# A decoder layer with routed experts on one core: leftover rows share three slots, and the orders of all engines are written anew

## The chip, the cores and the metric

The kernel runs on one core of one Trainium2 chip. The metric is device time in microseconds, the median of several runs; lower is better.

## The reference

The input x is 4 x 512 tokens of 512 channels. One layer computes three blocks, each followed by a layer norm over the channels.

```python
# block 1: a gated linear recurrence with quantised ("bitlinear") products
i = silu(bitlinear(x, Wi)) * (1 - f);  f = sigmoid(bitlinear(x, Wf))
h = scan over the tokens of a batch: h = f * h + i
o = rmsnorm(bitlinear(x, Wg)) * g_norm_weight * (h * sigmoid(h))
x = layernorm(x + bitlinear(o, Wo))
# block 2: each token goes to one of four experts, by its token id
e = min(token_id // 6250, 3)
x = layernorm(x + (silu(x @ ctx[e].T) * (x @ ctx[e].T)) @ ctx[e].T)
# block 3: eight square factors, which add up to one matrix
x = layernorm(x + (x @ sum_r factors[r]) / sqrt(8) + bias)
```

A bitlinear product rounds x per token to 8 bits and the weights to -1, 0 or 1. In block 2 the same matrix ctx[e] serves as gate, up and down weight.

## The kernel before

The 2048 tokens are 16 tiles of 128 rows, and 8 groups of two tiles. Block 1 runs group by group: `quantise_x`, `transpose_x`, three projections (`project_f`, `project_i`, `project_g`), the scans along the tokens on VectorE, `silu_h_by_token`, `output`, `quantise_o`, `transpose_o`, `project_back`, `residual_1`, `norm_1`. Then `scatter_rows` (GpSimd, an indirect DMA) writes each finished row with its token number to the DRAM array `sorted_rows`, at the row that `place` holds, so that the rows of one expert come to lie together.

Blocks 2 and 3 read `sorted_rows` slot by slot; a slot is 128 rows of one expert. As the four experts' row counts are no multiples of 128, the kernel has 19 slots (16 + 3). The first 13 (`SURE`) are always full. The last six may be part empty: they are first filled from `pad_row` by one large write, and rows that nothing was scattered to carry a token number out of bounds, so that `store` drops them. Which expert a slot has stands in `slot_off`, from which each expert product loads a register.

A slot n goes through: `load_rows` (SP queue; waits for the scatter of the groups that can reach it, the last group's for the last slots), `transpose_a` (PE), `high_a` and `low_a` (ACT and DVE split the transposed rows into a high and a low part), `up` (twelve matmuls 128x128 by 128x512: high by high, high by low, low by high), `silu_z` (ACT), `hidden` (DVE, silu(z) times z), `transpose_h`, `high_h`, `low_h`, `down` (twelve matmuls), `residual_2` (DVE), `square_2` (ACT), `power_2` (GpSimd), `norm_2` (ACT), `transpose_m`, `add_bias` (GpSimd), `high_m`, `low_m`, `mix` (twelve matmuls), `residual_3`, `square_3`, `power_3`, `norm_3`, and `store` (GpSimd, an indirect DMA to the output rows by token). The buffers for z, the hidden rows and the high and low parts exist once each; `rows` and `x2` are rings of four.

The routing is computed on the chip from the token ids at the start: counts per tile and expert by PE, running sums by DVE, and then `fill_events`, `number_slots`, `open_slots` and `places` as chains of small operations on GpSimd, each of which waits for the one before (`link`). `low_of_ctx` (DVE) and `high_of_ctx` (ACT) split the sixteen chunks of ctx; the first `up` waits for all sixteen.

The order of the work on each engine is written out by hand. The first groups are lists of calls. Three turns follow (groups 5 to 7 of block 1, with slots 3 to 8 beside them), then one turn with the last group's block-1 rest, and then the last stage, a loop over n from `TAIL` = 11 that issues up(n), transpose_a(n+1), transpose_m(n-2), down(n-1), transpose_h(n), mix(n-2). An engine works its list strictly in order, and semaphores hold it where an input isn't there or a buffer isn't free.

## Time and profile before

| what | value |
|---|---|
| median of 3 runs | 341.45 us (340.44 to 343.64) |
| profiled execution | 342.06 us |
| its span, first to last instruction | 340.3 us |
| PE busy | 278.1 us, 82% |
| DVE busy | 226.3 us, 66% |
| ACT busy | 229.6 us, 67% |
| POOL (GpSimd) busy | 190.8 us, 56% |
| mean granted clock of PE | 0.963 |

PE is the matmul engine (TensorE), PEld its weight load, which runs beside it. DVE is VectorE, ACT ScalarE, SP the engine that issues most DMAs. The span is a little shorter than the device time. A share of the whole span is an average over stages: which engine sets the pace has to be read stage by stage. In a timeline, the bracket behind an instruction tells how long its engine sat idle before it, and what ended that.

### The profile page before, as it was taken

Reading aid. Unit: us, or ns where it says so; the run is one execution under the profiler, and the core shown is the slowest. Engines: PE = TensorE matmul, PEld = TensorE weight load, DVE = VectorE, ACT = ScalarE, POOL = GpSimd, SP = SyncE. Lnnn points to the kernel's source line nnn. Section 1 sums busy time; section 2 is a strip of 40 time slices with the busy share of each in tenths; the row PEclk is TensorE's granted clock in tenths of the full one; section 3 lists DMA queues with packets and bytes.
Section 4 is the critical chain, followed back from the end, with each engine's and each line's share of the span. In section 5 each row is a group of like instructions: output and inputs, shape, how many; then the busy total and the mean of one; then the engine's idle time right before and its main releaser. Section 6 shows DMA issues by size and latency. Waiting matters only on the chain.

```text
span 340.3 us, 5734 instructions
## 1 busy us (share of the span) xinstructions
PE 278.1 (82%) x1505; PEld 211.9 (62%) x1518; DVE 226.3 (66%) x488; ACT 229.6 (67%) x456; POOL 190.8 (56%) x381
## 2 busy tenths in 40 slices
PE   1376646484879899999999998998999999999760
PEld 1253414252557678787778876676888888887540
DVE  2789999999987879968677696454543434543310
ACT  4687789889678769986887686476555644554530
...
DMA packets 17406, 37.02 MB, mean 109 GB/s; under 512 B 1503, under 2 KB 1631, under 8 KB 17376
## 3 DMA queue, kind: packets, MB, share of 16 engines
...
## 4 chain that ended last, share of the span: by engine, by line
PE 62%; ACT 9%; issue 5%; DVE 5%; DMA 2%; POOL 2%; ACTq 0%; POOLq 0%; DVEq 0%; SPq 0%
PE bank_y L1455 5%; PE bank_z L1455 5%; PE bank_y L1456 5%; PE bank_z L1456 5%; PE bank_z L1459 5%; PE bank_y L1459 5%; PE bank_m L1455 4%; PE bank_m L1456 4%; PE bank_m L1459 4%; PE bank_tr L1424 3%; PE bank_c L1357 2%; PE bank_q L1424 2%; PE bank_a L1357 1%; PE bank_b L1357 1%; DMA sorted_rows<-r,place 1%
## 5 line engine op out<-in xcount | busy, mean ns | idle before, releaser
L312 POOL TENSOR_SCALAR n_v<-n_dev 128x1 f32<-128x1 f32 (+1 forms) x46 | 8.8, 192 | 52.2 <-ACT x L644 26.7
L1455 PE MATMUL bank_y<-c_hi,h_hi 128*128 x76 | 31.8, 418 | 1.8 <-ACT h_hi L612 1.4
L996 DVE TENSOR_TENSOR act_z<-bank_z,act_z 128x512 f32<-128x512 f32 x19 | 13.1, 689 | 30.1 <-ACT act_z L626 30.1
L1455 PE MATMUL bank_m<-f_hi,m_hi 128*128 128x512 f32 x76 | 32.1, 423 | 0.8 <-ACT m_hi L612 0.8
L353 POOL TENSOR_TENSOR x<-x,bias_b 128x512 f32<-128x512 f32 x19 | 24.6, 1293 | 14.5 <-PE bank_q L1424 14.5
L1455 PE MATMUL bank_z<-c_hi,a_hi 128*128 x76 | 30.4, 400 | 2.8 <-ACT a_hi L612 1.5
L1456 PE MATMUL bank_m<-f_lo,m_hi 128*128 128x512 f32 x76 | 30.8, 405 | 0.0
L1456 PE MATMUL bank_y<-c_lo,h_hi 128*128 x76 | 30.1, 396 | 0.0
L1456 PE MATMUL bank_z<-c_lo,a_hi 128*128 x76 | 30.1, 395 | 0.0
L612 ACT ACTIVATE h_hi<-bank_tr 128x512 fp32r<-128x512 f32 x19 | 11.3, 596 | 26.7 <-PE bank_tr L1424 26.7
L313 POOL TENSOR_TENSOR n_d<-n_v,minus_half 128x1 f32<-128x1 f32 (+1 forms) x46 | 27.1, 588 | 3.8
L358 POOL DMA_INDIRECT out<-r,token_of x19 | 20.3, 1067 | 12.3 <-ACT r L651 7.6
L1013 DVE SCALAR_TENSOR_TENSOR r<-bank_m,x 128x512 f32<-128x512 f32 x19 | 13.1, 691 | 21.0 <-PE bank_m L1459 20.0
L1002 DVE SCALAR_TENSOR_TENSOR x<-bank_y,rows 128x512 f32<-128x512 f32 x19 | 13.1, 691 | 19.1 <-PE bank_y L1459 19.1
L638 ACT ACTIVATE x<-x,n_b,n_d 128x512 f32<-128x512 f32 x19 | 15.4, 810 | 12.2 <-POOL n_b L314 12.2
L1357 PE MATMUL bank_c<-xq_t,w_q 128*128 128x256 bf16 x128 | 18.3, 291 | 5.2 <-ACT mc_row L540 2.7
L343 POOL DMA_INDIRECT sorted_rows<-r,place x16 | 17.8, 1113 | 8.3 <-ACT r L594 5.7
L1459 PE MATMUL bank_m<-f_hi,m_lo 128*128 128x512 f32 x76 | 21.3, 403 | 0.0
L1459 PE MATMUL bank_y<-c_hi,h_lo 128*128 x76 | 20.6, 393 | 0.0
L1459 PE MATMUL bank_z<-c_hi,a_lo 128*128 x76 | 20.6, 393 | 0.0
L644 ACT ACTIVATE x<-r,n_mean 128x512 f32<-128x512 f32 x19 | 13.7, 720 | 9.6 <-DVE n_mean L1017 9.6
L626 ACT ACTIVATE act_z<-bank_z 128x512 f32<-128x512 f32 x19 | 11.2, 592 | 12.1 <-PE bank_z L1459 12.1
...
## 6 DMA issues: line engine op xcount, KB each, us to landing
...
```

The costliest lines, as they stand in the source:

```text
L313: link(pool.tensor_tensor(d, v, minus_half[:, 0:v.shape[1]], ALU.pow), chain)
L343: pool.indirect_dma_start(sorted_rows, bass.IndirectOffsetOnAxis(place[:, u:u + 1], 0), r1[:, j, :], None).then_inc(s_scat[j], 16)
L353: pool.tensor_tensor(tile, tile, bias_b[:], ALU.add).then_inc(s.x2b, 1)
L358: pool.indirect_dma_start(out_rows, bass.IndirectOffsetOnAxis(token_of[:, n:n + 1], 0), r3[:, n % 2, :], None, bounds_check=B * S - 1, oob ...
L638: a.activation(r, r, ACT.Identity, bias=n2_b[:, n % 2:n % 2 + 1], scale=n2_d[:, n % 2:n % 2 + 1]).then_inc(s.x2, 1)
L644: a.activation(x2[:, n % RING, :], r3[:, n % 2, :], ACT.Square, bias=n3_mean[:, n % 2:n % 2 + 1], accum_out=n3_dev[:, n % 2:n % 2 + 1]).th ...
L996: v.tensor_tensor(act_z[:], bank_z[:], act_z[:], ALU.mult).then_inc(s.hid, 1)
L1357: last = t.matmul(bank[:, i * GW:(i + 1) * GW], w_q[:, m, d, ch:ch + P], xq_t[:, :, d, :], start=(d == 0), stop=(d == KC - 1))
L1424: last = t.transpose(bank[:, c * P:(c + 1) * P], src[:, c * P:(c + 1) * P], ident[:])
L1455: t.matmul(bank[:], hi[:, c, :], w_hi(c), start=(c == 0), stop=False)
L1456: t.matmul(bank[:], hi[:, c, :], w_lo(c), start=False, stop=False)
L1459: last = t.matmul(bank[:], lo[:, c, :], w_hi(c), start=False, stop=(c == KC - 1))
```

## The change

The last six slots are replaced by three. Each of the three holds rows of two experts: GpSimd sorts the four leftover counts (`sort_left`), computes where each expert's leftover rows start and where they jump (`share_slots`), and which expert and which mask each of the six "units" has (`share_units`). There are then 16 slots and 19 units. A shared slot has one transpose_a, two ups, two hiddens with a mask per row, two transposes of h and two downs that add into one bank, and one residual_2, transpose_m and mix. The padding and its write are gone. Ahead of and behind that, the order of the calls is changed on all five engines, in the first groups and in the turns; the last stage is written out call by call. `sort_left` has 14 linked operations, `share_slots` 12, `share_units` 10, `places` 25 in place of 14. The diff follows, cut, in the order constants, SP, GpSimd, ACT, DVE, PE; of the orders of the first groups only stretches are shown.

```diff
-N_SLOTS = N_TILES + N_EXPERTS - 1
 SURE = N_TILES - N_EXPERTS + 1
+SHARED = N_TILES - SURE
+N_UNITS = SURE + 2 * SHARED
...
+def units_to(n):
+    return n + 1 if n < SURE else SURE + 2 * (n - SURE + 1)
+def slot_of(unit):
+    return unit if unit < SURE else SURE + (unit - SURE) // 2
+def is_last(unit):
+    return 0 <= unit < N_UNITS and units_to(slot_of(unit)) == unit + 1
...
-                sp.wait_ge(s.pad, 2)
-                sp.dma_start(sorted_rows[SURE * P:, :].rearrange("(k p) c -> p k c", p=P),
-                             pad_row[:, None, :].to_broadcast([P, N_SLOTS - SURE, ROW])).then_inc(s.padded, 16)
...
+                def sum_of_four(out, a, scratch):
+                    link(pool.tensor_tensor(scratch, a(slice(0, 2)), a(slice(2, 4)), ALU.add), s.route)
+                    link(pool.tensor_tensor(out, a(slice(0, 1)), a(slice(1, 2)), ALU.add), s.route)
+                def sort_left():
+                    expert = consts[:, 0:N_EXPERTS]
+                    square = [P, N_EXPERTS, N_EXPERTS]
+                    left = unsorted[:, 0, :]
+                    link(pool.tensor_scalar(unsorted[:, 1, :], expert, float(KC), None, ALU.mult), s.route)
+                    pool.wait_ge(s.left, 2)
+                    link(pool.tensor_scalar(sure_rows[:], sure_rows[:], float(P), None, ALU.mult), s.route)
+                    link(pool.tensor_tensor(left, through[:, :, N_TILES], sure_rows[:], ALU.subtract), s.route)
+                    link(pool.tensor_scalar(size_key[:], left, float(N_EXPERTS), None, ALU.mult), s.route)
+                    link(pool.tensor_tensor(size_key[:], size_key[:], expert, ALU.add), s.route)
+                    link(pool.tensor_tensor(pairs[:], size_key[:, :, None].to_broadcast(square),
+                                            size_key[:, None, :].to_broadcast(square), ALU.subtract), s.route)
+                    link(pool.tensor_scalar(pairs[:], pairs[:], 1.0, None, ALU.is_ge), s.route)
+                    sum_of_four(size_rank[:, :, None], lambda c: pairs[:, :, c], pairs[:, :, 0:2])
+                    link(pool.tensor_tensor(at_rank[:], size_rank[:, None, :].to_broadcast(square),
+                                            expert[:, :, None].to_broadcast(square), ALU.subtract), s.route)
+                    link(pool.tensor_scalar(at_rank[:], at_rank[:], 0.0, None, ALU.is_equal), s.route)
...
+                    sum_of_four(by_size[:, :, :, None], lambda c: sorted_pairs[:, :, :, c], sorted_pairs[:, :, :, 0:2])
+                def share_slots():
+                    square = [P, N_EXPERTS, N_EXPERTS]
+                    first, second, third = (by_size[:, k, 0:1] for k in range(3))
+                    link(pool.tensor_scalar(third_cut[:], second, -float(P), None, ALU.add), s.route)
+                    link(pool.tensor_scalar(third_over[:], third, P + 1.0, third, ALU.is_ge, ALU.mult), s.route)
+                    link(pool.tensor_scalar(jump[:], third, P + 1.0, third_cut[:], ALU.is_ge, ALU.mult), s.route)
+                    link(pool.tensor_scalar(base[:, 2:3], jump[:], SURE * P + 2.0 * P, None, ALU.add), s.route)
...
+                    sum_of_four(base_of[:, :, None], lambda c: pairs[:, :, c], pairs[:, :, 0:2])
+                def share_units():
+                    third, at = by_size[:, 2, 0:1], by_size[:, :, 1]
+                    link(pool.tensor_scalar(sizes[:, 0:2], by_size[:, 0:2, 0], 1.0, None, ALU.mult), s.route)
+                    link(pool.tensor_tensor(sizes[:, 2:3], third, jump[:], ALU.add), s.route)
+                    link(pool.tensor_scalar(shared_mask[:, 0:2 * SHARED:2], sizes[:], row_no, 1.0, ALU.subtract, ALU.is_ge),
+                         s.route)
...
+                    pool.tensor_scalar(shared_off[:], off_f[:], 1.0, None, ALU.mult).then_inc(s.shared, 1)
+                    pool.tensor_scalar(shared_mask[:, 1:2 * SHARED:2], shared_mask[:, 0:2 * SHARED:2], -1.0, 1.0, ALU.mult,
+                                       ALU.add).then_inc(s.shared, 1)
...
                     pool.wait_ge(s.next_fill, 6)
+                    link(pool.tensor_tensor(spare[:], through[:, :, 0:N_TILES], in_tile[:, 0, :, :], ALU.add), s.route)
                     link(pool.tensor_scalar(pos[:], filled[:, :, 0:N_TILES], -float(P), None, ALU.mult), s.route)
-                    link(pool.tensor_tensor(pos[:], pos[:], through[:, :, 0:N_TILES], ALU.add), s.route)
-                    link(pool.tensor_tensor(pos[:], pos[:], in_tile[:, 0, :, :], ALU.add), s.route)
+                    link(pool.tensor_tensor(pos[:], pos[:], spare[:], ALU.add), s.route)
                     link(pool.tensor_scalar(over[:], pos[:], float(P), None, ALU.is_ge), s.route)
                     link(pool.tensor_tensor(shift[:], later, now, ALU.subtract), s.route)
                     link(pool.tensor_scalar(shift[:], shift[:], float(P), -float(P), ALU.mult, ALU.add), s.route)
@@ -399,6 +477,20 @@
                     link(pool.tensor_scalar(placed[:], now, float(P), None, ALU.mult), s.route)
                     link(pool.tensor_tensor(placed[:], placed[:], pos[:], ALU.add), s.route)
                     link(pool.tensor_tensor(placed[:], placed[:], shift[:], ALU.add), s.route)
+                    wide = [P, N_EXPERTS, N_TILES]
+                    link(pool.tensor_tensor(spare[:], spare[:], sure_rows[:, :, None].to_broadcast(wide), ALU.subtract),
+                         s.route)
+                    link(pool.tensor_scalar(step[:], spare[:], jumps[:, 0:1], jumps[:, 1:2], ALU.is_ge, ALU.mult), s.route)
+                    link(pool.tensor_scalar(shared_at[:], spare[:], jumps[:, 2:3], jumps[:, 3:4], ALU.is_ge, ALU.mult), s.route)
+                    link(pool.tensor_tensor(step[:], step[:], shared_at[:], ALU.add), s.route)
+                    link(pool.tensor_tensor(step[:], step[:], at_rank[:, N_EXPERTS - 1, :, None].to_broadcast(wide), ALU.mult),
+                         s.route)
+                    link(pool.tensor_tensor(shared_at[:], spare[:], base_of[:, :, None].to_broadcast(wide), ALU.add), s.route)
+                    link(pool.tensor_tensor(shared_at[:], shared_at[:], step[:], ALU.add), s.route)
+                    link(pool.tensor_tensor(shared_at[:], shared_at[:], placed[:], ALU.subtract), s.route)
+                    link(pool.tensor_scalar(spare[:], spare[:], 0.0, None, ALU.is_ge), s.route)
+                    link(pool.tensor_tensor(shared_at[:], shared_at[:], spare[:], ALU.mult), s.route)
+                    link(pool.tensor_tensor(placed[:], placed[:], shared_at[:], ALU.add), s.route)
                     link(pool.tensor_tensor(placed[:], placed[:], chosen[:], ALU.mult), s.route)
...
                 number_slots()
+                open_slots()
                 weight_ready(W_F)
                 weight_ready(W_I)
-                open_slots()
+                sort_left()
                 weight_ready(W_G)
-                places()
-                add_factor(1)
+                share_slots()
                 scale_g(0)
                 power_x(2)
+                places()
                 scale_o(0)
+                add_factor(1)
                 weight_ready(W_O)
-                scale_g(1)
                 power_x(3)
                 number_rows(0)
...
-                scale_g(2)
+                share_units()
                 power_x(4)
...
                 square_x(1, 1)
                 weight_sum(W_F)
                 weight_sum(W_I)
+                max_row(0)
+                weight_sum(W_G)
+                weight_ready(W_F)
                 x_by_channel(0)
-                max_row(0)
-                weight_ready(W_F)
-                weight_sum(W_G)
                 weight_sum(W_O)
                 weight_ready(W_I)
                 tanh_f(0, 0)
-                forget(0, 0)
+                square_x(2, 0)
+                square_x(2, 1)
                 weight_ready(W_G)
                 silu_i(0, 0)
-                square_x(2, 0)
+                forget(0, 0)
+                high_of_ctx(0, range(0, 1))
+                tanh_f(0, 1)
                 square_g(0, 0)
+                silu_i(0, 1)
+                forget(0, 1)
+                max_row(1)
+                high_of_ctx(0, range(1, 2))
+                square_g(0, 1)
                 x_by_channel(1)
...
+                high_m(14)
+                square_3(13)
+                square_2(15)
+                norm_3(13)
+                square_3(14)
+                norm_2(15)
+                high_m(15)
+                norm_3(14)
+                square_3(15)
+                norm_3(15)
...
                     dve.wait_ge(s.sz, n + 1)
-                    v.tensor_tensor(act_z[:], bank_z[:], act_z[:], ALU.mult).then_inc(s.hid, 1)
+                    if n < SURE:
+                        v.tensor_tensor(act_z[:], bank_z[:], act_z[:], ALU.mult).then_inc(s.hid, 1)
+                    else:
+                        dve.wait_ge(s.shared, 2)
+                        v.scalar_tensor_tensor(act_z[:], bank_z[:], shared_mask[:, n - SURE:n - SURE + 1], act_z[:], ALU.mult,
+                                               ALU.mult).then_inc(s.hid, 1)
                 def residual_2(n):
                     i = slice(n % 2, n % 2 + 1)
-                    dve.wait_ge(s.y, n + 1)
+                    dve.wait_ge(s.y, units_to(n))
...
+                def sure_fills():
+                    dve.wait_ge(s.numbers, 1)
+                    v.scalar_tensor_tensor(sure_fill[:], number[:], float(SURE), gain[:], ALU.is_lt, ALU.mult
+                                           ).then_inc(s.left, 1)
+                    dve.wait_ge(s.left, 1)
+                    v.tensor_reduce(sure_rows[:], sure_fill[:].rearrange("p t e -> p e t"), AX, ALU.add).then_inc(s.left, 1)
...
+                quantise_x(2)
                 max_x(3, 0)
-                output(0, 0)
-                rescale_f(1, 0)
-                output(0, 1)
-                max_o(0, 0)
-                rescale_i(1, 0)
-                rescale_i(1, 1)
-                rescale_f(1, 1)
-                max_o(0, 1)
-                scale_x(2)
-                quantise_x(2)
-                round_weights(W_O)
+                weigh_g(1, 0)
+                scans(1, 0)
                 quantise_o(0)
-                gate_i(1, 0)
-                weigh_g(1, 0)
                 max_x(3, 1)
-                slot_offsets()
-                low_of_ctx([0])
-                scans(1, 0)
+                weigh_g(1, 1)
                 gate_i(1, 1)
-                low_of_ctx([1])
-                weigh_g(1, 1)
+                low_of_ctx([2])
+                scans(1, 1)
                 residual_1(0)
-                scans(1, 1)
+                low_of_ctx(range(3, 5))
                 rescale_f(2, 0)
...
+                residual_1(1)
+                output(2, 0)
+                rescale_f(3, 0)
+                rescale_f(3, 1)
+                output(2, 1)
...
                 residual_1(2)
+                low_of_ctx([13])
                 output(3, 0)
-                low_of_ctx(range(13, 15))
+                low_of_ctx([14])
+                max_x(5, 1)
+                low_of_ctx([15])
                 output(3, 1)
+                low_a(0)
                 rescale_f(4, 0)
-                max_x(5, 0)
-                low_of_ctx([15])
+                scale_x(5)
+                max_o(3, 0)
+                max_o(3, 1)
+                hidden(0)
...
+                def expert_product(unit, n, bank, hi, lo, s_hi, s_lo, s_done, first=True, last=True):
+                    if unit < SURE:
+                        off = slot_off[0:1, unit:unit + 1]
+                    else:
+                        pe.wait_ge(s.shared, 2)
+                        off = shared_off[0:1, unit - SURE:unit - SURE + 1]
+                    at = pe.value_load(off, min_val=0, max_val=(N_EXPERTS - 1) * KC)
                     product(n, bank, hi, lo, lambda c: flat(c_hi[:, bass.ds(at + c, 1), :]),
-                            lambda c: flat(c_lo[:, bass.ds(at + c, 1), :]), s_hi, s_lo, s_done)
+                            lambda c: flat(c_lo[:, bass.ds(at + c, 1), :]), s_hi, s_lo, s_done, first, last)
                 def up(n):
                     after(pe, s.hid, n)
@@ -1470,35 +1670,37 @@
                         pe.wait_ge(s.split_dve, N_EXPERTS * KC)
                         pe.wait_ge(s.slot_off, 1)
                         pe.wait_ge(s.o, GT * (MERGE - 1) + 1)
-                    expert_product(n, bank_z, a_hi, a_lo, s.tah, s.tal, s.z)
+                    expert_product(n, slot_of(n), bank_z, a_hi, a_lo, s.tah, s.tal, s.z)
                 def down(n):
-                    after(pe, s.r2, n)
-                    expert_product(n, bank_y, h_hi, h_lo, s.thh, s.thl, s.y)
+                    first = n < SURE or not is_last(n)
+                    if first:
+                        after(pe, s.r2, slot_of(n))
+                    expert_product(n, n, bank_y, h_hi, h_lo, s.thh, s.thl, s.y, first, is_last(n))
...
                 silu_h_by_token(3)
+                transpose_a(0)
                 project_f(4)
-                transpose_a(0)
+                up(0)
                 project_i(4)
-                up(0)
+                transpose_h(0)
                 project_g(4)
-                transpose_h(0)
                 pe.wait_ge(s.oqt, 3)
                 transpose_x(5)
-                spread_max(5)
                 pe.wait_ge(s.o, GT * MERGE)
                 down(0)
                 transpose_a(1)
+                spread_max(5)
                 pe.wait_ge(s.xqt, 6)
                 transpose_o(3)
                 up(1)
...
-                mix(TAIL - 3)
-                transpose_h(TAIL - 1)
-                transpose_a(TAIL)
-                for n in range(TAIL, N_SLOTS + 2):
...
+                mix(8)
+                transpose_a(11)
+                transpose_m(9)
+                transpose_h(10)
+                up(11)
+                transpose_a(12)
+                down(10)
+                transpose_h(11)
+                mix(9)
+                up(12)
+                transpose_a(13)
+                transpose_m(10)
+                down(11)
+                mix(10)
+                transpose_a(14)
+                transpose_h(12)
+                up(13)
+                transpose_m(11)
+                down(12)
+                transpose_h(13)
+                up(14)
+                mix(11)
+                down(13)
+                transpose_h(14)
+                transpose_m(12)
+                transpose_a(15)
+                up(15)
+                mix(12)
+                transpose_h(15)
+                down(14)
+                up(16)
+                down(15)
+                transpose_m(13)
+                up(17)
+                transpose_h(16)
+                mix(13)
+                down(16)
+                transpose_h(17)
+                up(18)
+                down(17)
+                transpose_h(18)
+                transpose_m(14)
+                down(18)
+                mix(14)
+                transpose_m(15)
+                mix(15)
```

## Rows read from the trace of the kernel before

**Rows 1.** Busy time by stage: length, busy PE, PEld, DVE, ACT, POOL; clock, DMA share, GB/s.
```profile
27.00:97.20 70.20, 43.16 (x281) 26.79 (x283) 68.86 (x140) 59.78 (x128) 47.66 (x82) 0.90 0.80 182
97.20:237.60 140.40, 134.68 (x746) 104.39 (x755) 100.60 (x212) 104.19 (x212) 88.63 (x183) 1.00 0.28 79
237.60:308.50 70.90, 70.90 (x350) 58.39 (x351) 31.43 (x74) 37.23 (x72) 32.05 (x65) 1.00 0.15 51
308.50:340.30 31.80, 18.22 (x76) 13.59 (x74) 7.63 (x20) 11.38 (x21) 12.99 (x23) 0.82 0.03 10
```

**Rows 2.** The same view for one slot of the last stage.
```profile
249.40:259.08 9.68, 9.68 (x50) 7.99 (x49) 4.29 (x10) 5.22 (x10) 4.48 (x9) 1.00 0.18 57
```

**Rows 3.** The chain that ended last (start, us, what), steady last stage.
```profile
246.61 0.94 PE bank_m L1459 x4
249.40 0.93 PE bank_z L1459 x4
```

**Rows 4.** The same chain, where the last group's rows come back from memory.
```profile
229.30 3.94 DMA sorted_rows<-r,place
233.32 2.62 DMA rows<-sorted_rows
236.16 0.67 PE bank_a L1424 x4
```

**Rows 5.** The chain again, in the drain behind the last up product.
```profile
307.57 0.93 PE bank_z L1459 x4
...
324.86 0.47 PE bank_m L1455
328.08 1.38 PE bank_m L1459 x4
```

**Rows 6.** Timeline of PE at up(11) (start, us, engine, line, operation; idle before it).
```profile
237.60 0.49 PE L1455 MATMUL bank_z<-c_hi,a_hi 128*128 x1 [0.78 <-ACT a_hi L612]
```

**Rows 7.** The chain at unit 1: silu, then hidden.
```profile
110.78 0.61 ACT act_z L626
111.41 0.70 DVE act_z L996
```

**Rows 8.** Timeline of PE in the first 120 us.
```profile
49.39 1.89 PE L1419 MATMUL bank_m<-w_q,oq_t 128*128 128x512 bf16 x4 [1.48 <-DVE slot_off L1085]
...
97.19 0.49 PE L1455 MATMUL bank_z<-c_hi,a_hi 128*128 x1 [1.33 <-issue]
...
107.70 0.49 PE L1455 MATMUL bank_z<-c_hi,a_hi 128*128 x1 [0.36 <-ACT a_hi L612]
...
112.16 0.66 PE L1424 MATMUL bank_tr<-small,act_z 128*128 128x128 f32 x4 [0.98 <-DVE act_z L996]
```

**Rows 9.** Timeline of ACT: the second square of g in group 0.
```profile
34.81 0.59 ACT L561 ACTIVATE squares<-bank_b 128x512 bf16<-128x512 f32 x1
```

**Rows 10.** Timeline of POOL in the first 70 us.
```profile
28.84 0.38 POOL L392 TENSOR_SCALAR pos<-filled 128x64 f32<-128x64 f32 x1 [1.25 <-DVE slot_at L1080]
29.30 0.31 POOL L393 TENSOR_TENSOR pos<-pos,through 128x64 f32<-128x64 f32 x1
...
30.10 0.81 POOL L395 TENSOR_SCALAR over<-pos 128x64 f32<-128x64 f32 x1
...
35.98 0.20 POOL L405 CAST place<-place_f 128x16 int32<-128x16 f32 x1
...
42.51 1.93 POOL L282 TENSOR_TENSOR o_rc<-o_mc,minus_one 128x2 f32<-128x2 f32 x1
...
62.89 0.21 POOL L277 TENSOR_TENSOR o_v<-o_ms,g_u 128x2 f32<-128x2 f32 x1
...
64.75 0.72 POOL L282 TENSOR_TENSOR o_rc<-o_mc,minus_one 128x2 f32<-128x2 f32 x1
```

**Rows 11.** Timeline of DVE: quantising o of group 0, the last low part.
```profile
45.76 1.70 DVE L902 TENSOR_SCALAR o_tok<-o_tok,o_q 128x512 f32<-128x512 f32 x2
...
94.97 0.68 DVE L1022 TENSOR_TENSOR c_lo<-c_stage,c_hi 128x512 fp32r<-128x512 f32 x1
```

681 lines of the change are left out of this document (383 added, 298 removed).

## The prediction

> **What bounds the kernel now.** I read the busy time by stage first [rows 1]. The reader is to see four regimes. From 27 to 97 us VectorE (DVE) is busy 68.86 of 70.20 us and TensorE (PE) only 43.16: DVE sets the pace. From 97.2 to 237.6 us PE is busy 134.68 of 140.40, and from 237.6 to 308.5 us it never stops (70.90 of 70.90, granted clock 1.00). In the last 31.80 us PE works 18.22: one slot's chain of dependences is left over. So PE work saved behind 97 us shortens the kernel one for one, and each microsecond DVE loses ahead of 97 us delays everything behind it.
>
> In the steady last stage a slot takes 9.68 us, all PE [rows 2]. One product of twelve matmuls takes 249.40 - 246.61 = 2.79 us [rows 3]. Three products are 8.37, so the three groups of four transposes take 9.68 - 8.37 = 1.31, or 0.44 each.
>
> **Part 1, three mixes fewer.** Up and down products stay 19 each (13 sure slots, and two experts in each of three shared ones). Three times a transpose of a, a transpose of m and a mix go: 3 x (2.79 + 2 x 0.44) = 11.0 us of PE. It comes out in two places.
> - From the first read of slot 11 (236.16 [rows 4]) to the end of the last up (307.57 + 0.93 = 308.5 [rows 5]) there are 22 products and 22 groups of transposes before, 20 and 18 after: -(2 x 2.79 + 4 x 0.44) = -7.3. The new order puts the transposes of m(9) and h(10) between transpose a(11) and up(11), which fills the 0.78 us of [rows 6]: together -8.1.
> - From 308.5 to the end at 340.3 one product and one group of transposes go: -3.2. Against it, norm_2(15) is now issued behind square_3(14), which waits for mix(14), although its own inputs come earlier: I add 0.3. The last mix runs from 324.86 to 328.08 + 1.38 = 329.46, 4.60 us where others take 2.79, after a wait [rows 5]; the granted clock of the stage is 0.82 [rows 1]. The new one stands behind a similar wait, and I keep 4.60. Together -2.9.
>
> The tail gives -11.0. Does its new order stall? One unit needs, between its up and its down, silu and hidden (0.61 + 0.70 and their waits, about 1.4 [rows 7]), a transpose, and the two splits of the same shape (about 1.3). The order has a product of 2.79 us over each: down(n-1) or a mix over silu and hidden, the next up over the splits. I walked units 11 to 18 with these durations and found one wait of 0.2 us. ACT and DVE have room (5.22 and 4.29 of 9.68 [rows 2]). The masked multiply in hidden has the shape of the plain one, and costs the same. SP must load slot 15 after token_of_row(11), which POOL now does behind power_2(12): the load lands about 2 us before its transpose. The register load ahead of each product is covered by four queued transposes; without that cover it costs up to the 1.33 us of [rows 8].
>
> **Part 2, the routing on POOL.** sort_left is 14 small operations, share_slots 12, share_units 10, and places grows from 14 to 25: 47 more, each waited for. sort_left stands in the gap ahead of weight_ready(W_G), where DVE is rounding that weight: nothing. share_slots stands before scale_g(0), which must wait for the second square of g anyway (34.81 [rows 9]): nothing. share_units comes near 70 us, where POOL waits for residual 1: nothing. Without that cover these three cost 36 x 0.39 (the shortest row and its gap) = 14 us on POOL.
>
> places is the exposed one: it now stands between power_x(2) and scale_o(0), where it was ahead of both. Its 14 operations took 35.98 + 0.20 - 28.84 = 7.3 us, 0.52 each; a 128x64 operation takes between 0.31 and 0.81 [rows 10]. Bounds for eleven more: 11 x 0.39 = 4.3 and 11 x 0.90 = 9.9; I take 0.52, the mean of their own neighbours, 5.8. So places takes 13.1, and 1.7 more as DVE rounds W_O meanwhile: in that stretch before, o_rc took 1.93 instead of 0.72 [rows 10]. It starts near 35.1 (the squares of g, then power_x(2)) and ends at 49.9; scale_o(0) needs 64.75 + 1.0 - 62.89 = 2.9, so o's scale is there at 52.8.
>
> The Trainium skill (SBUF — State Buffer, "SBUF: two separate sides") says that VectorE and GpSimd share one port pair under an exclusive lock, the loser being blocked for the whole operation. The trace agrees for o_rc (1.93 against 0.72). Taken for every operation of places, the rule gives about 350; with the neighbours' mean, the sum below.
>
> **Part 3, the front's new order.** quantise_o(0) began on DVE at 45.76 [rows 11]. The new order puts 4.2 us more in front of it (gate 0.6, two scans 1.3, a weighing 0.6, two low parts 1.2, slot offsets 0.1, sure_fills 0.4), so DVE arrives at 50.1 and waits for 52.8: +2.7 (bounds 0 and 7). Behind it: project_back(0) needs POOL's half of W_O, which now follows scale_o(0) and add_factor(1), hence starts near 55.5, and its two halves take 1.9 and 1.5 [rows 8]: DVE waits 1.0 in residual_1(0). output(2,0) now follows residual_1(1) directly, where a rescale stood between, and waits for PE's transposes: 0.8. Up to the last low part of ctx, which ended at 95.65 [rows 11] and releases up(0), the DVE work is 0.2 shorter (one more max_x and sure_fills; one output and one rescale fewer). DVE lag: 2.7 + 1.0 + 0.8 - 0.2 = 4.3.
>
> PE: up(0) moves ahead of project_i(4), 8 + 8 matmuls of 0.87 us a half, which used to run while PE waited for that low part: +1.75 of work behind the gate. In return it and the new order fill waits of 0.36 and 0.98 [rows 8]: -1.3. The front costs 4.3 + 1.75 - 1.3 = +4.75. In 97 to 237 us I change nothing: the same work, PE idle 5.7 in all; the gate by the last group's rows (3.94 + 2.62 us of DMA [rows 4]) moves along.
>
> The 1.5 MB of padding written at the start go, and with them a wait of scatter_rows(0) that was long over: 0, for nothing in the PE or DVE waits names that transfer.
>
> **Sum.** Span 340.3 - 11.0 + 4.75 = 334.05. The profiled execution took 342.06, 1.76 outside its span: 335.8. The median shown (341.45) is 0.6 below it: 335.2.
>
> **Rivals.** A measurement of this kernel can tell about 1% from no change.
> - A, the front absorbs the routing. places runs at its lower bound and nothing collides (POOL 4 us earlier, oq_s before DVE arrives), and the two later waits vanish with it. Then the front costs about 0.3, and the span is 340.3 - 11.0 + 0.3 = 329.6: 330.8. If the last mix also keeps the full clock, 329. For it: DVE has no other wait in [rows 1]'s second stage. Against: W_O behind add_factor is in the order.
> - B, the shared stage stalls. Units of one slot share act_z, bank_z, bank_tr and h, each single; if the register load shows at half of the 12 products of the shared units (6 x 1.33 = 8.0 less the 2 of lag it could absorb), the time is about 341. For it: 1.33 us stood bare before up(0) [rows 8]. Against: no gap at all in 22 products of the last stage [rows 1].
> - C, slower. The lock: every operation of places, and share_slots ahead of it, takes 0.92 with its gap (0.81 and up was seen [rows 10]). places then takes 23.0 instead of 13.1 and share_slots pushes its start by 12 x 0.53 less 1.5 of slack, 4.9: DVE waits 14.8 longer, and the time is 350. It decides from 6 us over my value, where the gain is used up.
> - That the saved work isn't on the path: excluded by 70.90 of 70.90 [rows 1].
>
> **How the numbers follow.** The forecast as told (331.8 to 338) 0.52, A 0.25, cases between it and no change (B, or half of C) 0.15, C or B in full, beyond 1% slower, 0.08. So faster 0.78, same 0.14, slower 0.08. The range takes in A with the full clock and B: 328.5 to 341.
>
> **What would show it.** Right: 16 mixes and 38 expert products; up(0) near 101 to 102 instead of 97.2; a DVE wait for POOL's o_q of 2 to 3 us before quantise_o(0); PE without gap from the first read of slot 11 to the last up, in about 64 us instead of 72.3; about 29 us from there to the end. Wrong in the front: up(0) at 98 or before. Wrong in the tail: PE gaps before bank_z or bank_y in the last 50 us, released by h_hi, act_z or nothing visible. The forecast falls if the middle stage loses more than it did before, for which I have no row.

## The result, and the profile after

The changed kernel takes 343.33 us (median of 20 runs, 340.92 to 346.41), the kernel before 341.51 us beside it (20 runs): a ratio of 1.0052, 95% interval 1.0032 to 1.0072. The forecast was 335.2 us in a range of 328.5 to 341, faster with a chance of 0.78. It was wrong: the change gains nothing and loses about 1.8 us. The times are medians of all executions; the ratios and their 95% intervals leave out executions that took over 1.5% longer than a kernel's fastest.

One thing has to be known before the trace is read. The profiled execution of the changed kernel took 341.05 us (span 339.2), 2.3 us under its own median, and the profiled one of before 342.06, 0.6 over its own. By the two traces the changed kernel is 1.1 us shorter, by the medians 1.8 us longer. So the trace shows where the forecast failed, but some 3 us of the loss at the median lie outside what it can show. The record has one thing on them. The mean granted clock of PE over an execution goes with the time: the six longest executions of the changed kernel (344.8 to 346.4 us) have 0.914 to 0.920, the six shortest (340.9 to 342.2) 0.923 to 0.946, and before has 0.963 in its profiled execution and 0.95 at the median of its later ones. Where in the kernel the clock differs, and whether it makes the time or follows it, no run shows.

The busy time by stage of the changed kernel (length, busy PE, PEld, DVE, ACT, POOL, clock, DMA share, GB/s); the cuts are up(0), transpose a(11) and about the last down product. The first stage answers to the first one of [rows 1]; the second ends at transpose a(11), where the one in [rows 1] goes on to up(11), so the stretch to hold beside it is 236.16 - 97.19 = 138.97:

```profile
27.00:103.77 76.77, 43.82 (x271) 27.25 (x269) 70.18 (x140) 59.05 (x123) 59.13 (x116) 0.82 0.57 137
103.77:245.33 141.56, 135.11 (x763) 104.76 (x763) 100.12 (x211) 104.80 (x212) 89.00 (x180) 1.00 0.29 78
245.33:316.80 71.47, 70.91 (x345) 58.08 (x346) 27.78 (x61) 30.83 (x60) 25.70 (x51) 1.00 0.11 38
316.80:339.20 22.40, 7.88 (x28) 5.55 (x27) 3.25 (x10) 6.08 (x11) 8.03 (x15) 0.72 0.09 35
```

The reader is to see that up(0) comes at 103.77 instead of 97.19 [rows 8], that DVE, which had 1.3 us idle in the front's stage [rows 1], has 6.6 now, and that PE still never stops for long in the 71 us from transpose a(11) on.

The chain that ended last, at the last group's rows and in the drain (start, us, what; it answers to [rows 4, 5]):

```profile
238.76 3.65 DMA sorted_rows<-r,place
242.49 2.79 DMA rows<-sorted_rows
245.33 0.66 PE bank_a L1619 x4
...
308.85 0.93 PE bank_z L1654 x4
...
323.54 0.76 PE bank_m L1650
327.06 0.95 PE bank_m L1654 x4
```

From transpose a(11) to the end of the last up product it is 309.78 - 245.33 = 64.45 us, where it was 308.5 - 236.16 = 72.34 [rows 4, 5]: -7.9. From there to the end it is 29.4 us for 31.8: -2.4. The saving is all there. Transpose a(11) itself comes at 245.33 instead of 236.16, 9.2 us later: 6.6 of it up to up(0), 2.6 in the stage between.

The same chain between the front and up(1) shows a path that before's chain doesn't take:

```profile
105.55 6.39 DMA sorted_rows<-r,place
112.00 2.67 DMA rows<-sorted_rows
...
116.65 0.49 PE bank_z L1650
```

The scatter of group 2 takes 6.39 us where the last group's took 3.65; an accumulate of the factors was issued at 98.49, 7 us ahead of it. PE had other work meanwhile and stood 0.70 us for these rows and 0.61 before up(1), so in this trace the path costs PE at most 1.3 us.

DVE's timeline in the front (start, us, engine, line, operation, and in brackets the idle time before it and what ended it), the answer to [rows 11]:

```profile
22.97 0.69 DVE L1069 TENSOR_TENSOR t_ch<-bank_c,mc_row 128x512 f32<-128x512 f32 x1 [1.46 <-PE bank_c L1552]
24.67 0.69 DVE L1069 TENSOR_TENSOR t_ch<-bank_a,mc_row 128x512 f32<-128x512 f32 x1 [1.02 <-PE bank_a L1552]
...
54.32 0.91 DVE L1057 TENSOR_SCALAR o_tok<-o_tok,o_q 128x512 f32<-128x512 f32 x2 [2.97 <-POOL o_q L304]
...
60.82 0.75 DVE L1123 SCALAR_TENSOR_TENSOR r<-bank_tr,o_a,xs 128x512 f32<-128x512 f32 x1 [0.55 <-PE bank_tr L1614]
...
79.91 0.69 DVE L1107 TENSOR_TENSOR o_tok<-o_tok,bank_z 128x512 f32<-128x512 f32 x1 [0.86 <-PE bank_z L1598]
...
91.95 0.97 DVE L1057 TENSOR_SCALAR o_tok<-o_tok,o_q 128x512 f32<-128x512 f32 x2 [1.49 <-POOL o_q L304]
...
101.75 0.68 DVE L1182 TENSOR_TENSOR c_lo<-c_stage,c_hi 128x512 fp32r<-128x512 f32 x1
```

The three waits that were forecast are there, nearly to size (2.97, 0.55 and 0.86 for 2.7, 1.0 and 0.8). Three that were not are there too: 1.46 and 1.02 at the first rescales, 1.49 at quantise_o(2). POOL's timeline shows the stretch of places, and what stood before quantise_o(2) (it answers to [rows 10]):

```profile
37.62 0.31 POOL L470 TENSOR_TENSOR spare<-through,in_tile 128x64 f32<-128x64 f32 x1
...
42.92 3.04 POOL L484 TENSOR_SCALAR shared_at<-spare,jumps 128x64 f32<-128x64 f32 x1
...
51.43 0.20 POOL L497 CAST place<-place_f 128x16 int32<-128x16 f32 x1
...
85.61 1.40 POOL L327 DMA_DIRECT2D f_sum<-in_factors  x1 [1.50 <-DMA f_sum<-in_factors]
...
88.11 2.41 POOL L300 TENSOR_TENSOR o_mf<-o_max,o_r 128x2 f32<-128x2 f32 x1
```

places took 51.63 - 37.62 = 14.0 us where 14.8 were forecast, though it began 2.5 us later. Two steps of 0.2 and 0.6 us stretch to 2.4 and 3.0 where DVE issues several operations back to back.

### The profile page after: what moved, and what is told of

The parts are those of the page before. It is cut to its first block, busy times and chain, and to the rows that moved or that the text cites. A ratio compares the mean times of both kernels' runs of the same rounds, so it can differ in the third digit from the quotient of the medians.

```text
span 339.2 us, 5554 instructions
## 1 busy us (share of the span) xinstructions
PE 267.8 (79%) x1458; PEld 203.7 (60%) x1458; DVE 218.4 (64%) x466; ACT 217.8 (64%) x432; POOL 198.6 (59%) x401
## 4 chain that ended last, share of the span: by engine, by line
PE 56%; POOL 17%; DMA 9%; issue 7%; ACT 5%; DVE 4%; SPq 0%; POOLq 0%; DVEq 0%; ACTq 0%
PE bank_z L1650 5%; PE bank_y L1650 5%; PE bank_z L1654 5%; PE bank_y L1654 5%; PE bank_z L1651 5%; PE bank_y L1651 5%; PE bank_m L1650 4%; PE bank_m L1651 4%; PE bank_m L1654 4%; PE bank_tr L1619 4%; DMA sorted_rows<-r,place 3%; DMA f_sum<-in_factors 3%; DMA xs<-in_x 2%; DMA rows<-sorted_rows 2%; PE bank_c L1552 2%
## 5 line engine op out<-in xcount | busy, mean ns | idle before, releaser
L373 POOL TENSOR_TENSOR x<-x,bias_b 128x512 f32<-128x512 f32 x16 | 20.6, 1286 | 14.1 <-PE bank_q L1619 14.1
L1650 PE MATMUL bank_m<-f_hi,m_hi 128*128 128x512 f32 x64 | 27.1, 424 | 0.8 <-ACT m_hi L728 0.8
L333 POOL TENSOR_TENSOR n_d<-n_v,minus_half 128x1 f32<-128x1 f32 (+1 forms) x40 | 23.9, 598 | 3.4
L1651 PE MATMUL bank_m<-f_lo,m_hi 128*128 128x512 f32 x64 | 25.9, 404 | 0.0
L378 POOL DMA_INDIRECT out<-r,token_of x16 | 17.3, 1081 | 12.8 <-ACT r L767 7.2
L1162 DVE SCALAR_TENSOR_TENSOR x<-bank_y,rows 128x512 f32<-128x512 f32 x16 | 11.0, 689 | 20.0 <-PE bank_y L1654 20.0
L1138 DVE TENSOR_TENSOR m_lo<-bank_q,m_hi 128x512 fp32r<-128x512 f32 x16 | 11.0, 689 | 16.4 <-ACT m_hi L728 16.4
L1650 PEld LDWEIGHTS bank_z<-c_hi,a_hi 128*128 128x128 f32 x76 | 14.3, 188 | 7.4 <-issue 4.6
L1138 DVE TENSOR_TENSOR h_lo<-bank_tr,h_hi 128x512 fp32r<-128x512 f32 x19 | 13.0, 686 | 8.2 <-ACT h_hi L728 8.2
L1650 PEld LDWEIGHTS bank_y<-c_hi,h_hi 128*128 128x128 f32 x76 | 14.3, 188 | 6.5 <-issue 3.5
```

The source lines that it names most:

```text
L333: link(pool.tensor_tensor(d, v, minus_half[:, 0:v.shape[1]], ALU.pow), chain)
L373: pool.tensor_tensor(tile, tile, bias_b[:], ALU.add).then_inc(s.x2b, 1)
L378: pool.indirect_dma_start(out_rows, bass.IndirectOffsetOnAxis(token_of[:, n:n + 1], 0), r3[:, n % 2, :], None, bounds_check=B * S - 1, oob ...
L1138: v.tensor_tensor(flat(lo[:]), bank[:], flat(hi[:]).bitcast(F32), ALU.subtract).then_inc(s_done, 1)
L1650: t.matmul(bank[:], hi[:, c, :], w_hi(c), start=(first and c == 0), stop=False)
L1651: t.matmul(bank[:], hi[:, c, :], w_lo(c), start=False, stop=False)
```

## The experiments

Two explanations are held against each other. **Theory 1**: GpSimd's added steps and the accumulates of the factors that they push back cost the front what it lost. **The order**: the new lists that came with the change cost by themselves (in the expectations of old_front_new_pool, no_share and no_share_old this is the other case, or the rival). Theories 2 and 3 in two expectations are smaller ones, on the accumulates and on one wait, and are told with their runs. Each kernel is timed against the kernel before on its own chip. In the tables "up(0)" and "a(11)" are the starts of the first up product and of transpose a(11) in the profiled execution; before has 97.2 and 236.2, the changed kernel 103.8 and 245.3. From a(11) to the end of the span all kernels with the new end took 93.9 to 95.5 us, so the two columns hold most of what the traces differ by; the medians can differ by more.

### Moving single things within the changed kernel

**places_split**: the last 15 steps of places behind scale_g(1).

```diff
                 power_x(3)
                 number_rows(0)
                 scale_g(1)
+                places_b()
```

> The changed kernel with one thing moved: the last fifteen operations of places run behind scale_g(1), not ahead of scale_o(0). Theory 1: the DVE wait of 2.97 us before quantise_o(0) goes (o's scale is there near 50 at the latest), and later waits decide: 1.5 us for o's scale in group 2 stays. up(0) near 101 to 102 instead of 103.8, ratio to before about 0.995. If the places chain doesn't matter because other waits are behind it, ratio as the changed kernel, 1.005.

Measured: 343.63 us, ratio 1.0041 (1.001 to 1.0072); up(0) 104.2, a(11) 246.5. The wait at quantise_o(0) went, as theory 1 has it, but quantise_o(1) now waited 2.4 us, the wait at quantise_o(2) rose to 2.3, and residual 1 waited 1.1 us for the scatter. Nothing was won: what leaves one wait arrives at the next.

**factor_later**: one accumulate of the factors (1 MB) behind scale_o(2), right ahead of scatter_rows(1).

```diff
-                add_factor(4)
                 scale_o(2)
+                add_factor(4)
                 scatter_rows(1)
```

> The changed kernel with add_factor(4) behind scale_o(2). In the changed kernel GpSimd stood 1.5 us at add_factor(4), for the DMA of the factor before, and then 2.4 us in one operation of scale_o(2) under a run of DVE operations with two SBUF inputs; DVE waited 1.5 us for the result. Theory 1: with scale_o(2) issued first its operation lies ahead of that run, the DVE wait goes, up(0) 1.5 to 2.5 us earlier, ratio to before about 0.999 to 1.000. Rival: another wait stands right behind (rows of slot 0 or PE), and less than 0.5 us is won.

Measured: 352.29 us, ratio 1.0309 (1.0255 to 1.0364); up(0) 114.4. The chain shows it:

```profile
91.44 1.49 POOL f_sum L327
93.23 1.12 POOL sorted_rows L363
94.66 8.24 DMA sorted_rows<-r,place
102.99 7.19 DMA rows<-sorted_rows
110.22 1.12 PE bank_tr L1619 x4
```

Scatter and load of the rows take 15.4 us where the last group's took 3.94 + 2.62 [rows 4]. DVE stood 5.8 us for that scatter at the next residual 1. An accumulate issued right ahead of them costs some 9 us over the changed kernel: one line in the list is worth as much as the whole change.

**factors_early**: every accumulate one place earlier, none ahead of scale_o(2).

```diff
+                add_factor(1)
                 scale_g(0)
                 power_x(2)
                 places()
                 scale_o(0)
-                add_factor(1)
+                add_factor(2)
...
-                add_factor(4)
                 scale_o(2)
```

> The changed kernel with the accumulates of the factors each one place earlier on GpSimd's queue: the first leaves ahead of places at 35 us in place of 54.5, the second at 54, the third at 65, the fourth at 75, and none ahead of the second group's output scale at 85.6, where GpSimd waited 1.50 us, or beside the scatter of group 1. Theory 2 (the late chain of 1 MB accumulates is what delays the start of the expert stage): up(0) 2 to 3 us earlier, 338 to 341 us. Rival (the accumulates are only passengers, the cost is GpSimd's and VectorE's own work): 342.5 to 344 us, up(0) at 103 to 104 us.

Measured: 343.0 us, ratio 1.0029 (0.9995 to 1.0063); up(0) 104.6, a(11) 245.5. The wait at quantise_o(2) is gone and the one at quantise_o(0) is 4.1 us for 2.97. The rival's time was right, and the accumulate ahead of scale_o(2) was a passenger. The run doesn't clear the one ahead of scatter_rows(2): it still leaves at 99.18, and the scatter behind it still takes 6.30 us.

**low_apart**: three low parts behind quantise_o(2).

```diff
-                low_of_ctx(range(8, 11))
                 quantise_o(2)
+                low_of_ctx(range(8, 11))
```

> The changed kernel with the three low parts of the context that stand ahead of quantise_o(2) set behind it. Theory 3 (three low parts back to back with the gate hold GpSimd's o_mf for 2.4 us, which is the 1.49 us wait of quantise_o(2)): quantise_o(2) starts 1 to 2 us earlier and group 1 and 2 with it, 341.5 to 342.5 us. Rival (the last low parts are what up(0) waits for, and their sum stays): 343 to 344 us.

Measured: 342.36 us, ratio 0.9999 (0.9964 to 1.0034); up(0) 104.8, a(11) 244.8. The mechanism of theory 3 held:

```profile
88.60 0.25 POOL L300 TENSOR_TENSOR o_mf<-o_max,o_r 128x2 f32<-128x2 f32 x1
90.29 0.97 DVE L1057 TENSOR_SCALAR o_tok<-o_tok,o_q 128x512 f32<-128x512 f32 x2 [1.49 <-POOL o_q L304]
```

o_mf takes 0.25 us where it took 2.41, and quantise_o(2) starts at 90.29 instead of 91.95. DVE's wait there is 1.49 as before, since DVE, without the low parts, arrives earlier too; and up(0) is no earlier, as the rival has it: the low parts still have to be done. The plain medians, 342.36 against 341.13, give a ratio of 1.0036. The interval reaches into that of the changed kernel, and it isn't a shown gain.

### The added steps under the order of before

**old_front_new_pool**: the lists of before for ACT, DVE and PE in the front, and for all engines in the turns; POOL's front as changed.

```diff
 ACT, DVE, PE: lists of before, sure_fills behind weight_scale(W_I)
 POOL: list of the changed kernel; turns of before
```

> As the kernel before in the calls of ACT, DVE and PE up to slot 10, with the changed kernel's order on GpSimd in the first groups (places between power_x(2) and scale_o(0)), and the new last stage. If GpSimd's new order alone makes the front slow, the old order of the others, which wants o's scale at 45.8, waits longer than the new one did: DVE waits 6 to 8 us before quantise_o(0), up(0) at 104 to 106, ratio 1.00 to 1.02. If the new order of ACT, DVE and PE makes it slow, up(0) is at 99 to 101 and the ratio 0.98 to 0.99.

Measured: 351.04 us, ratio 1.0251 (1.0201 to 1.03); up(0) 111.7, a(11) 255.5. The wait before quantise_o(0) is there with 5.8 us, a little under the forecast; up(0) is 6 us later than either case allowed, and DVE also waits 4.7 us for ACT's i_ch at 94.6 us.

**old_front2**: the lists of before on all engines, the added steps set into POOL's waits.

```diff
                 number_slots()
+                sort_left()            # nine of its steps
                 weight_ready(W_F)
+                sort_left_b()
+                open_slots()
                 weight_ready(W_I)
-                open_slots()
+                share_slots()
                 weight_ready(W_G)
                 places()               # its first ten steps
                 add_factor(1)
...
                 scale_g(1)
+                places_b()             # the other fifteen
```

> The order lists of the kernel before, front and turns, on all engines, with the changed kernel's end; the added scalar steps of GpSimd are set where it waited for the weights' rounding and behind group 1's gate, the last 15 steps of places behind scale_g(1), and the first accumulate of the factors leaves at 36 us as before. Theory 1 (GpSimd's added steps in front of group 0's output quantiser, with the accumulates of the factors pushed back behind them, cost the front): up(0) comes back to 97 to 99 us and the time to 331 to 334 us. Rival 1 (the added steps cost wherever they stand, since GpSimd is held by VectorE's port anyway): up(0) at 101 to 104 us, 337 to 343 us. Rival 2 (the changed order of ScalarE, VectorE and TensorE is itself needed by the shorter end): the middle stage stays at 141.5 us, the time at 336 to 340 us.

Measured: 343.59 us, ratio 1.0083 (1.0055 to 1.0111); up(0) 109.4, a(11) 247.7. Theory 1's forecast fails, and rival 1 fits better, though up(0) is later than it said too: with the lists of before the steps cost 12.2 us at up(0), though they were put into POOL's waits. DVE's timeline shows the first of it, in a gap that had looked free:

```profile
24.28 0.69 DVE L1076 TENSOR_TENSOR t_ch<-bank_c,mc_row 128x512 f32<-128x512 f32 x1 [3.87 <-PE bank_c L1560]
```

The largest others are 3.21 us for power_x(3), which stands behind places_b, and 1.27 and 2.99 for ACT's i_ch.

**before_plus11**: the kernel before with eleven more steps of 128x64 in places, and nothing else.

```diff
                 placed = placed + shift
+                extra[0] = placed * chosen
+                ten more of the same shape, each waited for
                 placed = placed * chosen
```

> The kernel before, with eleven more linked operations of 128x64 in places, whose result nobody reads: about 11 x 0.55 = 6 us more on GpSimd at 35 us, nothing else changed. If GpSimd's length there passes to the end one for one: 346 to 348 us, up(0) at 102 to 103 us. If only what is over the slack passes (1.9 us of wait at the first output scale and 5.6 us of idle time behind it): 342 to 345 us. If the slack takes it all: 341.5 us.

Measured: 344.92 us, ratio 1.0109 (1.007 to 1.0147); up(0) 101.7, a(11) 240.1. The 11 steps took 4.6 us of POOL (35.20 to 39.78) where 6 were expected, and they move up(0) by 4.5 and the time by 3.7 us: nearly one for one. Waits and idle time of POOL on both sides (over 7 us) took in little of it. The time lies in the range of the second case, but the slack is not what made it so.

**spread** and **spread2**: the same lists of before, with the steps spread from 22 to 67 us, and scatter_rows(0) behind scale_o(1). spread2 differs in the accumulates alone (and power_x(3) and power_1(0) moved up).

```diff
                 weight_ready(W_I)
                 open_slots()
+                sort_left()
                 weight_ready(W_G)
+                sort_left_b()
...
                 weight_ready(W_O)
+                share_slots()
...
+                places_b()
+                places_c()
                 scale_o(1)
+                add_factor(3)          # spread2; spread: behind power_x(4)
                 scatter_rows(0)
...
+                add_factor(4)          # spread2
                 scale_o(2)
                 scatter_rows(1)
-                add_factor(4)          # spread
```

> All the computation of the changed kernel, with the order of the kernel before on ScalarE, VectorE and TensorE (front and turns) and the changed kernel's end. The added steps stand where GpSimd has nothing due: the sort behind open_slots and behind W_G's half, share_slots and the last fifteen steps of places in the stretch from 47 to 64 us, scatter_rows(0) behind group 1's output scale, share_units behind the last scatter of the front; the accumulates leave at about 36, 51, 72, 86, 100, 108 and 117 us. If what the changed kernel lost is the changed order of the lists, and the added steps can be hidden: up(0) at 98 to 101 us, middle stage 138.5, 332 to 336 us, and it beats both kernels. If GpSimd's added steps cost wherever they stand (old_front2 had up(0) at 109.4): 339 to 344 us.

> As spread, with the accumulates of the factors kept away from the loads of the sorted rows (in spread two left at 90.2 and 105.5 us, right behind a scatter, and the rows' load behind each took 7.3 and 7.5 us for 2.7): they leave at about 37, 56, 71, 82, 96, 111 and 121 us, and power_x(3), for which VectorE waited 2.6 us, comes ahead of scale_g(1). If spread's 149.9 us between up(0) and transpose a(11) came of those collisions and of the seventh accumulate at 133.7 us: middle 138.5 to 141, up(0) 101 to 102.5, total 335 to 339 us. If it came of the added steps' delay of the scatters: middle 145 and more, total over 342 us.

Measured: spread 349.52 us, ratio 1.0257 (1.0224 to 1.029), up(0) 102.4, a(11) 252.3. Its chain, behind accumulates at 90.2 and 105.5 us:

```profile
92.92 7.27 DMA rows<-sorted_rows
...
108.05 7.51 DMA rows<-sorted_rows
```

spread2 343.94 us, ratio 1.0048 (1.0015 to 1.008), up(0) 108.4, a(11) 247.9: the stage behind up(0) is back to 139.5 us, as forecast by the collisions, but up(0) is 6 us later, which neither case had. The largest of DVE's waits up to there (line, what it waited for, total, times, longest):

```profile
DVE r L1134 <- DMA sorted_rows<-r,place: 6.8, 2, 6.4
```

Residual 1 of the second group overwrites the one buffer that the first group's scatter reads. In spread, with the same steps ahead of that scatter but no accumulate since 54.7 us, the wait isn't there. In spread2 the moved accumulate stands right ahead of it, and its chain has:

```profile
71.34 1.54 POOL f_sum L327
...
75.72 8.57 DMA sorted_rows<-r,place
```

So the accumulates collide in spread2 too, at another place. Three placements under the old lists end at 247.7, 247.9 and 252.3 for a(11); that the steps can't be placed better there is not shown.

### The order without the added steps

**no_share** leaves out all sharing steps (its rows go to the places of their own numbers, mask and offsets are constants, so its output is another); **sort_only** and **place_only** keep one half; **no_share_old** is no_share with the lists of before.

```diff
-                sort_left()            # no_share, place_only
-                share_slots()          # no_share, place_only
-                sure_fills()           # no_share, place_only
-                eleven steps of places # no_share, sort_only
-                share_units()          # no_share, sort_only
+                pool.tensor_copy(place[:], numbers).then_inc(s.place, 1)
```

> The changed kernel with all the steps left out that place rows in shared slots: sort_left, share_slots, the eleven added steps of places, share_units and VectorE's sure_fills; the mask and the experts' offsets of the shared slots are constants, and every row is written to the place of its own number, so rows are not sorted by expert and the output is another. Everything else, the order lists of all engines too, is that of the changed kernel. Theory 1 (GpSimd's added steps are what the front lost): up(0) at 96 to 98 us, the time 334 to 337 us, lower than the kernel before by the whole gain of the tail less what the later accumulates cost. Rival (the changed order of the lists is what the front lost): up(0) at 101 to 104 us, 341 to 344 us.

> As no_share, but sort_left, share_slots and sure_fills are kept (28 GpSimd steps between 19 and 35 us, ahead of and between the halves of the rounded weights) and only the eleven steps of places and share_units are left out. If the early steps cost by the halves of the weights coming late (the 1.46 and 1.02 us of rescale_f(0)): 2 to 3 us over no_share, 337 to 339 us. If it is the late ones alone that cost: as no_share.

> As no_share, but the eleven steps of places and share_units are kept (with constants for what the sort gives) and sort_left, share_slots and sure_fills are left out. If the late steps cost by group 0's output quantiser (2.97 us in the changed kernel) and by the accumulates behind them: 3 to 4 us over no_share, 338 to 341 us. If the quantiser's wait was only reached because the early steps had pushed places back: within 1 us of no_share.

> As no_share, with the order lists of the kernel before on all engines for the front and the turns, and the changed kernel's end. This is the front of before with the shorter tail and nothing added: up(0) at 97 us, 329 to 332 us. The difference to no_share is what the changed order costs or gives by itself: theory 1 says 2 us or less either way; a rival, in which the changed order costs, says 6 us and more.

| kernel | time, us | ratio to before (95%) | up(0) | a(11) |
|---|---|---|---|---|
| no_share | 340.18 | 0.9930 (0.9904 to 0.9955) | 102.7 | 244.8 |
| sort_only | 339.01 | 0.9894 (0.9863 to 0.9926) | 102.5 | 244.7 |
| place_only | 341.27 | 0.9967 (0.9934 to 1.0000) | 101.8 | 244.4 |
| changed | 343.33 | 1.0052 (1.0032 to 1.0072) | 103.8 | 245.3 |
| no_share_old | 331.36 | 0.9661 (0.9623 to 0.9698) | 97.7 | 236.0 |

The old order with the shorter end gives 331.36 us, in its forecast of 329 to 332. The new order gives 340.18 without a single added step: 8.8 us between two medians of one chip, and 0.9930 - 0.9661 is 9.2 us of 341.5, where theory 1 allowed 2. The steps add 1.0052 - 0.9930, 4.2 us. And -11.6 + 9.2 + 4.2 = +1.8. Either half of the steps alone moves the ratio by less than the intervals tell apart.

Two limits belong to this. First, the 4.2 us of the steps are in the medians and hardly in the traces: a(11) is at 244.8 without them and 245.3 with them, and the profiled executions took 340.78 and 341.05. Second, order and steps don't add up independently:

| | without the steps | with the steps |
|---|---|---|
| lists of before | 0.9661 (no_share_old) | 1.0048 (spread2, the lowest of four) |
| new lists | 0.9930 (no_share) | 1.0052 (changed) |

Under the lists of before the same steps cost 13 us and more, and with the steps in, the new lists cost nothing against them. So the order is a cause by itself, shown without the steps; but taking the order back doesn't give its 9.2 us back, because the steps then cost that much more.

Busy time up to the end of the last low part (columns as above), of before, no_share_old, no_share and the changed kernel:

```profile
27.00:95.65 68.65, 42.94 (x280) 26.78 (x282) 67.31 (x138) 58.23 (x124) 46.58 (x81) 0.90 0.79 181
```

```profile
27.00:96.28 69.28, 45.71 (x274) 28.59 (x278) 66.95 (x137) 58.21 (x124) 48.48 (x81) 0.80 0.67 152
```

```profile
27.00:101.50 74.50, 45.89 (x259) 28.71 (x264) 66.96 (x136) 57.12 (x121) 44.85 (x80) 0.75 0.60 140
```

```profile
27.00:102.43 75.43, 43.31 (x268) 27.03 (x266) 68.84 (x138) 57.80 (x121) 58.83 (x115) 0.82 0.57 137
```

DVE does the same 67 us of work in the first three. (The changed kernel has 68.84, because its two late first rescales push work behind 27 us: from 20 to 27 us its DVE was busy 4.45 us, that of no_share 6.23.) DVE is idle 1.3 and 2.3 us in the old order, and 7.5 in the new one with POOL at its least busy; in the changed kernel it is 6.6. The waits of DVE in that window of no_share:

```profile
DVE o_tok L1092 <- PE bank_z L1582: 2.3, 2, 1.9
DVE o_tok L1042 <- POOL o_q L306: 1.5, 1, 1.5
DVE r L1108 <- PE bank_m L1598: 1.1, 1, 1.1
DVE r L1108 <- PE bank_tr L1598: 0.9, 1, 0.9
```

The longest stand at output(2,0), quantise_o(2) and residual_1(0), close behind what their inputs are made from. Those at output(2,0) and residual_1(0) had been forecast for the changed kernel, and rival A let both vanish if places were quick. They are there without the steps, and longer: 1.92, and 1.06 and 0.86 us.

### Which part of the order

**ns_front_old_turns_new**, **ns_first27_old** and **ns_half_old** are no_share with parts of the lists of before; **old_turns** and **old_turns_first27** are the same cuts in the complete kernel.

```diff
-front of no_share, all engines     +front of before (ns_front_old_turns_new)
-first 8 PE, 15 ACT, 21 DVE, 8 POOL +those of before (ns_first27_old)
-first 32 PE, 77 ACT, 57 DVE, 19 POOL +those of before (ns_half_old)
-turns of the changed kernel        +turns of before (old_turns)
-turns, first 8 PE, 15 ACT, 21 DVE  +those of before; POOL: W_F, W_I, open_slots,
                                     W_G, sort_left, share_slots (old_turns_first27)
```

> The sharing steps left out as in no_share (rows written to the places of their own numbers, constants for mask and offsets); front lists of the kernel before on all engines, turns of the changed kernel. no_share_old gave 331.4 and no_share 340.2 us, 5.0 us apart at up(0) and 3.8 us in the stage from there to transpose a(11). If the turns' new order is what the middle stage lost: up(0) at 97.7, middle 141 to 142, 334.5 to 335.5 us. If the middle stage lost it by what the front left over (work moved behind up(0)): middle 138 to 139, 331 to 332.5 us.

> As no_share, but the first section alone of the lists (to about 27 us: 21 entries of VectorE, 15 of ScalarE, 8 of TensorE and 8 of GpSimd) in the order of the kernel before. If the front lost its 5 us there (the rounded weights and the first rescale come later in the new order): up(0) at 98 to 100 us, 335 to 338 us. If it lost them later, in the interleaving of groups 1 to 3: up(0) at 102 to 103 us, 339.5 to 340.5 us.

> As no_share, but the lists of the kernel before up to gate_i(1, 1) and weigh_g(1, 1) on VectorE (57 entries), 77 of ScalarE, 32 of TensorE, 19 of GpSimd, and the changed order behind them. If the loss lies in groups 0 and 1: up(0) near 98 to 99 us, 335 to 337 us. If it lies in what comes last before up(0) (project_f(4), and the low parts of the context bunched up): up(0) at 101 to 103 us, 338 to 340 us.

> The changed kernel, complete, with the turns alone in the order of the kernel before (front and end as changed). ns_front_old_turns_new was 2.5 us over no_share_old; if that is the turns' own price: 340 to 341 us, the stage between up(0) and transpose a(11) 139 to 140 us for 141.5. If it hung on the old front: 343 us.

> As old_turns, and the first section of the lists (to about 27 us) in the order of the kernel before, the halves of the rounded weights ahead of open_slots, sort_left and share_slots on GpSimd, behind W_G's half. ns_first27_old had up(0) 2.3 us earlier than no_share. If the first rescales' waits (1.46 and 1.02 us) were what the front lost first: up(0) at 101 to 102 us, 338 to 339.5 us. If the same steps only come later to group 0's output quantiser: up(0) at 103.5 to 105 us, 340.5 to 343 us.

| kernel | time, us | ratio to before (95%) | up(0) | a(11) |
|---|---|---|---|---|
| ns_front_old_turns_new | 333.89 | 0.9783 (0.9743 to 0.9823) | 98.3 | 239.3 |
| ns_first27_old | 339.82 | 0.9948 (0.9925 to 0.9972) | 100.4 | 243.0 |
| ns_half_old | 340.99 | 0.9987 (0.9962 to 1.0012) | 101.6 | 243.8 |
| old_turns | 344.60 | 1.0039 (1.0004 to 1.0073) | 105.1 | 248.5 |
| old_turns_first27 | 347.65 | 1.0119 (1.0057 to 1.018) | 107.8 | 249.8 |

The loss lies in both parts: the old front under new turns gains 5.0 us of 9.2 over no_share (0.9930 - 0.9783), the old turns under the old front the other 4.2, each uncertain by more than 1 us; at a(11) the traces divide it into 5.5 and 3.3. But no part of the front gives its share alone. The first 27 us in the old order bring up(0) 2.3 us forward and the median not at all; with half of the front up(0) is 1.1 us earlier and the ratio no better (0.9987), and at the seam DVE waits 4.04 us for ACT's i_ch, a wait that neither whole order has. In the complete kernel the old turns gain nothing measurable, and the old beginning costs 2.7 us more: share_slots stands behind W_G's half in both, but sort_left and open_slots come later, and DVE's wait at quantise_o(0) is 4.97 us where old_turns has 3.30. What the turns lose by themselves stays partly open: in the profiled execution of ns_front_old_turns_new one stretch also shows a granted clock of 0.88 where the others have 1.00, and that execution took 336.05, over its median.

```profile
210.30:224.30 14.00, 11.99 (x53) 8.58 (x54) 5.28 (x12) 5.24 (x11) 6.87 (x14) 0.88 0.26 94
```

No order that was tried with the steps complete beats the kernel before.

## Why the prediction was wrong

- **Part 1, three mixes fewer: right.** -11.0 forecast; the trace gives -7.9 and -2.4, together -10.3. Per piece -8.1 and -2.9 were forecast. no_share_old has it on the clock: -11.6 us by its ratio, -10.9 between the medians. PE ran 70.91 of 71.47 us, with no wait there for a register load, so rival B fell.
- **Part 2, places: right in size.** 14.0 us for 14.8, and the wait at quantise_o(0) 2.97 for 2.7. But the wait is worth less than its length: no_share has none there and up(0) only 1.1 us earlier, as other waits take its place.
- **Part 2, "sort_left stands in the gap ... nothing": right in the new lists, not in the old ones.** sort_only keeps sort_left and share_slots and is no slower than no_share. The two waits at the first rescales (1.46 and 1.02 us) come ahead of sort_left, which begins at 22.17: four steps of number_slots and open_slots take 1.26 to 1.35 us there, two of them 0.33 in no_share, and place_only has both waits without sort_left. They vary between kernels of one list (factors_early has 0.56 us in all). In the old lists the same steps in "gaps" aren't free: in old_front2 four of them take 1.08 to 1.27 us beside DVE's rounding, W_F's half starts at 21.19 instead of 17.91, and DVE waits 3.87.
- **Part 3, the front's new order: the step that failed.** The prediction sums the DVE lag from three waits (2.7 + 1.0 + 0.8, the first two behind places), less 0.2 for shorter DVE work, and takes the rest of the new sequence as neutral. The work is equal (66.96 and 66.95 us), but the new sequence leaves DVE waiting 7.5 us instead of 2.3 with no added step at all, and up(0) then comes 5.0 us later. In the trace of the changed kernel the lag at up(0) is 6.6 for 4.3. Only these few places of the new list were walked.
- **"In 97 to 237 us I change nothing": wrong.** It took 2.6 us more in the trace, and no_share, without the steps, loses 3.8 us there against no_share_old. 1.75 of it was forecast, as project_i(4) behind up(0), and counted in the front. The waits that were to fill against it (-1.3) hardly did: a_hi before up(1) still costs 0.61 (0.36 in [rows 8]) and act_z 0.8 (0.98), and over the stage the waits for h_hi grew from 1.4 to 1.9 us and those for a_hi from 0.7 to 1.6. Up to a(11) the forecast has 4.3 + 1.75 - 1.3 = 4.75, the trace 9.2.
- **The median.** The forecast put it 0.6 us below the profiled execution; it lies 2.3 above. These 2.9 us no trace explains.
- **Rivals.** A (the front absorbs the routing) was seen in no order: no_share_old comes down to its time, but has no added routing in it. C, the lock, was overrated for places: single steps took 3.04 and 2.41 us, but the mean of its 25 was 0.56. The forecast's own condition came true: it "falls if the middle stage loses more than it did before".

Put as a sum from the ratios, along this one path: -11.6 (end) + 4.2 (turns' order, behind the old front) + 5.0 (front's order) + 4.2 (steps, in the new lists) = +1.8. The front and the stage behind it together were forecast at +4.75 and cost 13.4 by the ratios, 9.2 of them by the order alone. Which of the many moved calls makes the order slow stays open.
